# Two PSUM banks in turn for the last products of an expert slot, and a wait for the copy two slots behind

## The chip, the cores and the metric

The kernel runs on one core of a Trainium2 chip. Time is microseconds of one execution on the device. It is given as the median of three runs, and one further execution was profiled. TensorE is PE in the rows, VectorE DVE, ScalarE ACT, GpSimd POOL and SyncE SP.

## The reference, cut to what matters

Eight layers run over 4096 tokens of 128 numbers: a state-space layer, experts, landmark attention, the same experts again, causal attention, another set of experts, attention with a memory, and those experts again. The change touches the four expert layers. With 8 experts (the first two of them) each token takes two experts, with 4 experts (the last two) it takes one:

```python
g = jnp.einsum('bsh,ehi->ebsi', x, experts_w1)
u = jnp.einsum('bsh,ehi->ebsi', x, experts_w3)
hid = jax.nn.silu(g) * u                       # 512 numbers for a token and an expert
eo = jnp.einsum('ebsi,eih->ebsh', hid, experts_w2)
out = jnp.einsum('ebsh,bse->bsh', eo, tok_w)
```

## The kernel before

`expert_layer` computes only what the routing asks for. It sorts the tokens by expert into **slots** of 128 rows, each slot of one expert. An upper bound on their number is fixed: 71 slots in each of the first two expert layers, 35 in each of the last two, 212 in all. All numbers are fp32. Each engine has its own program and runs it in order. Semaphores tie them together. For slot n:

- POOL `gather(n)` (L575): an indirect DMA brings 128 token rows from DRAM into `xs`, six buffers deep. POOL issues the gather of slot n + 6 and then the scatter of slot n.
- PE `turn_rows(n)` (L725): one transpose of those rows into PSUM bank 4, issued two slots ahead. ACT `turned_rows` (L636) copies it to `xst`. ACT `up_weights(n)` (L649) copies the weights of the slot's expert, 128x1024, to `up_w`.
- PE `up(n)` (L733): the gate half into bank 0 or 1 and the other half into bank 2 or 3, four products of 128x128 each. The trace shows two matmul instructions for a product, so 16 for a slot.
- ACT `silu(n)` (L642) reads the first half, DVE `hidden(n)` (L856) multiplies it by the second into `hid`, two buffers deep.
- PE `rows(n)` (L741): the **last products**, 8 matmul instructions that add up in PSUM bank 5, columns 0 to 127. The semaphore `y_ready` tells of the last of them.
- DVE `rows(n)` (L862) copies bank 5 to one of four buffers `ys` and raises `y_copied`. Before it, DVE waits until the scatter of four slots back has landed (L861).
- POOL `scatter(n)` (L580) waits for `y_copied` and writes the rows to DRAM by an indirect DMA.

PE's order in its loop over n is: the waits for slot n's operands (`xst_ready`, `silu_ready` of slot n - 2, `up_copied`), the gate half, the other half, the transpose for slot n + 2, and the last products of slot n - 1. DVE's order is `hidden(n)`, then the copy of slot n - 1. ACT's order is `silu(n)`, the copy of the turned rows of slot n + 2, the weights of slot n + 2. When all slots are done, SP waits for the scatters, loads the results, and they are added to the tokens.

Banks 6 and 7 of the tensor `ps` hold the routing's numbers, which are all read before the first slot. In the slot loop they are unused.

Of the kernel before, what the change touches and what calls it, by code (L numbers as in the profile page):

```python
# [12 lines left out]
P = 128  # L13
# [417 lines left out]
def expert_layer(nc, g, name, experts, top, weights, gate_w, up_of, down, result=None):  # L431
# [8 lines left out]
    IB = 4  # L440
# [8 lines left out]
    XS, YS, WS = 6, 4, 3  # L449
    with ExitStack() as ctx:  # L450
# [16 lines left out]
        tiles, done, start = s.sb("tiles", [P, E]), s.sb("done", [P, E]), s.sb("start", [P, E])  # L467
# [14 lines left out]
        sg, hid = s.sb("sg", [P, 2, CHUNK]), s.sb("hid", [P, 2, CHUNK])  # L482
        up_w = s.sb("up_w", [P, WS, 2 * CHUNK])
        ys = s.sb("ys", [P, YS, P])
# [4 lines left out]
        ps = s.ps("ps", [P, 8, 512])  # L489
# [8 lines left out]
        S = {n: s.sem(n) for n in names}  # L498
# [19 lines left out]
        with nc.Block() as block:  # L518
# [151 lines left out]
            def _(pe):  # L670
# [39 lines left out]
                for k in range(K):  # L710
# [5 lines left out]
                    last = nc.tensor.matmul(ps_sums[:, k // NT, :], signs[:, k, :], coded[:, k, :], start=(k % NT == 0), stop=(k % NT == NT - 1))  # L716
# [10 lines left out]
                def expert_of(n):  # L727
                    return nc.values_load(table_e[0:1, n:n + 1], engines=(mybir.EngineType.PE,), min_val=0, max_val=E - 1,
                                          skip_runtime_bounds_check_because="table_e counts the experts that end before a slot and is cut at E - 1 by VectorE")
# [5 lines left out]

                def rows(n, e):
                    pe.wait_ge(S["hid_ready"], n + 1)
                    if n:
                        pe.wait_ge(S["y_copied"], n)
                    for j in range(IB):  # L740
                        last = nc.tensor.matmul(ps[:, 5, 0:P], hid[:, n % 2, j * P:j * P + P], down(e, j), start=(j == 0), stop=(j == IB - 1))  # L741
                    last.then_inc(S["y_ready"], 1)

                pe.wait_ge(S["table_ready"], 1)
# [2 lines left out]
                e, before = expert_of(0), None  # L747
                for n in range(SLOTS):
                    pe.wait_ge(S["xst_ready"], n + 1)
                    if n >= 2:  # L750
                        pe.wait_ge(S["silu_ready"], n - 1)
                    pe.wait_ge(S["up_copied"], n + 1)
                    up(n, 0, n % 2).then_inc(S["g_ready"], 1)
                    if n >= 2:
                        pe.wait_ge(S["hid_ready"], n - 1)
                    up(n, CHUNK, 2 + n % 2).then_inc(S["u_ready"], 1)
                    after = expert_of(n + 1) if n + 1 < SLOTS else None
                    if n + 2 < SLOTS:
                        turn_rows(n + 2)
                    if n:  # L760
                        rows(n - 1, before)
                    before, e = e, after
                rows(SLOTS - 1, before)

            @block.vector
            def _(dve):
# [3 lines left out]
                for c in range(NC_):  # L770
                    for t in range(c * CT, c * CT + CT):
                        last = nc.vector.tensor_scalar(xn[:, t, :], g.X[:, t, :], g.MV[:, t, 0:1], rstd[:, t:t + 1], ALU.subtract, ALU.mult)
# [35 lines left out]
                for r in range(top):  # L808
                    last = nc.vector.tensor_tensor(place[:, r], hot[:, r], rank[:].rearrange("p e t -> p t e"), ALU.mult)
# [48 lines left out]
                def rows(n):  # L858
                    dve.wait_ge(S["y_ready"], n + 1)
                    if n >= YS:  # L860
                        dve.wait_ge(y_stored[n % YS], n // YS * 16)  # L861
                    nc.vector.tensor_copy(ys[:, n % YS, :], ps[:, 5, 0:P]).then_inc(S["y_copied"], 1)  # L862

                hidden(0)
                for n in range(1, SLOTS):
                    hidden(n)
                    rows(n - 1)
                rows(SLOTS - 1)

                def fold(c):  # L870
# [1521 lines left out]
```

## Time and profile before

| | us |
|---|---|
| median of three runs | 2788.8 |
| lowest and highest | 2781.56, 2790.41 |
| the profiled execution, its own time | 2790.66 |
| span of that execution, first to last instruction | 2788.9 |
| PE busy (matmul), share of the span | 2227.6, 80% |
| DVE, ACT, POOL busy | 1813.1, 1398.5, 897.8 |
| mean granted clock of TensorE | 0.884 |

A busy time is the union of an engine's records. The four stretches in which the slot loops run are a quarter of the span; what the change does is read there. A duration of a matmul in the rows is from its start to its modelled end, and matmuls overlap: where they follow each other without a gap, one starts every 0.11 us or so, though each has 0.275 us in its record. So work on PE is better counted by starts than by busy time.

### The profile page before, as it was taken

To read this page: it belongs to the slowest core of one execution; us is meant where nothing else is said; L and a number is where in the kernel's file an instruction comes from. 1 tells how busy PE (TensorE), PEld (TensorE's weight loads), DVE (VectorE), ACT (ScalarE), POOL (GpSimd) and SP (SyncE) were. 2 spreads that over 40 slices of the span, in tenths; PEclk is the share of its full clock that TensorE was granted. 3 is DMA by queue.
4 is the path that set the end of the run, shared out by engine and by line. 5 is a ranking of instruction groups with operands and counts; after the bars stand their busy time and mean duration, and the time that the engine had idled before them with its cause. 6 is when DMAs were issued, how large, how long until landed. Compare 5 with 4: busy or idle time off the path is not lost. (4 is left out here: it accounts for less than half of the span.)

```text
span 2788.9 us, 78885 instructions
## 1 busy us (share of the span) xinstructions
PE 2227.6 (80%) x30447; PEld 1572.1 (56%) x30447; DVE 1813.1 (65%) x5841; ACT 1398.5 (50%) x3584; POOL 897.8 (32%) x904
## 2 busy tenths in 40 slices
PE   6499947699935888888888877948899888888686
PEld 3288835388812333333333335836777777777486
DVE  6633357633355776767867634359999999999622
ACT  5455543455521554454544445536556555555453
POOL 2156643166541101000000003534444444444254
PEclk7699979699965998988988887969999999999898
DMA  4111120111143211110110001121111111111112
GB/s 125 36 41 42 43 70 1 39 42 42 42 139 93 63 31 35 33 43 18 43 33 22 15 1 52 42 82 53 52 51 53 48 49 50 45 49 49 40 39 89
DMA packets 76684, 134.93 MB, mean 48 GB/s; under 512 B 17892, under 2 KB 32926, under 8 KB 73886
## 3 DMA queue, kind: packets, MB, share of 16 engines
q1 hardware_dynamic: 62742, 102.07, 11.6%
q0 software_dynamic: 13568, 27.81, 3.4%
q8 instruction: 250, 4.10, 0.6%
q14 instruction: 116, 0.95, 0.1%
q10 hardware_dynamic: 8, 0.00, 0.0%
HBM read 65.19 MB, written 32.79 MB: 35 GB/s over the span
## 5 line engine op out<-in xcount | busy, mean ns | idle before, releaser
L1499 ACT ACTIVATE ca_pt<-ca_ps 128x512 f32<-128x512 f32 (+3 forms) x768 | 341.9, 491 | 402.2 <-PE ca_ps L1601 198.8
L733 PE MATMUL ffn_ps<-ffn_xst,ffn_up_w 128*128 128x128 f32 x3392 | 420.6, 278 | 0.2 <-issue 0.2
L733 PEld LDWEIGHTS ffn_ps<-ffn_xst,ffn_up_w 128*128 128x128 f32 x3392 | 402.7, 195 | 1.2 <-issue 1.2
L856 DVE TENSOR_TENSOR ffn_hid<-ffn_sg,ffn_ps 128x512 f32<-128x512 f32 x212 | 145.8, 688 | 324.8 <-PE ffn_ps L733 234.3
L580 POOL DMA_INDIRECT ffn_y<-ffn_ys,ffn_result_at x212 | 208.8, 985 | 221.6 <-DVE ffn_ys L862 190.4
L1928 POOL TENSOR_TENSOR im_pt_e<-im_pt,im_own 128x512 f32<-128x512 f32 x128 | 162.6, 1271 | 361.9 <-DVE im_pt L2181 351.6
L575 POOL DMA_INDIRECT ffn_xs<-ffn_x,ffn_token_at x212 | 205.2, 968 | 229.7 <-DVE ffn_token_at L839 166.3
L1575 PE MATMUL ca_ps<-ca_stacks 72*128 72x512 bf16 (+3 forms) x768 | 233.3, 371 | 53.8 <-DVE ca_m_near L1721 28.2
L1597 PE MATMUL ca_ps<-ca_stacks 75*128 75x512 bf16 (+3 forms) x768 | 259.5, 361 | 16.8 <-ACT ca_pt L1499 11.2
L1720 DVE TENSOR_REDUCE ca_m_far<-ca_ps 128x1 f32<-128x128 f32 (+5 forms) x384 | 236.8, 617 | 49.7 <-PE ca_ps L1575 48.0
L1721 DVE CUSTOM_DVE_ANT_0 ca_spill<-ca_ps,ca_bias_q 128x256 f32<-128x256 f32 (+1 forms) x512 | 201.0, 397 | 32.5 <-PE ca_ps L1575 32.5
L1619 PE MATMUL ca_ps<-ca_pt,ca_vp 128*9 128x512 f32 (+3 forms) x1536 | 184.5, 555 | 41.6 <-ACT ca_ysb L1507 41.6
L642 ACT ACTIVATE ffn_sg<-ffn_ps 128x512 f32<-128x512 f32 x212 | 126.4, 596 | 139.4 <-PE ffn_ps L733 130.0
L1935 POOL TENSOR_TENSOR im_rope_qk<-im_t,im_mates 128x512 f32<-128x512 f32 x128 | 173.8, 1358 | 62.6 <-DMA im_mates<-im_t 61.7
L543 POOL MEMSET ffn_gate_wide<- 128x32 f32 x4 | 0.5, 125 | 593.4 <-POOLq L42 593.4
L741 PE MATMUL ffn_ps<-w_w,ffn_hid 128*128 x1136 | 156.3, 281 | 34.2 <-DVE ffn_ys L862 33.9
L1734 DVE TENSOR_TENSOR ca_ps<-ca_ps,ca_bias_kd 128x256 f32<-128x256 f32 (+1 forms) x288 | 109.9, 382 | 103.9 <-PE ca_ps L1597 100.0
L1575 PEld LDWEIGHTS ca_ps<-ca_stacks 72*128 72x128 bf16 x768 | 68.7, 104 | 191.1 <-DVE ca_m_near L1721 97.8
L862 DVE COPY ffn_ys<-ffn_ps 128x128 f32<-128x128 f32 x212 | 61.7, 291 | 161.0 <-remote 122.4
L741 PEld LDWEIGHTS ffn_ps<-w_w,ffn_hid 128*128 128x128 f32 x1136 | 137.8, 191 | 48.9 <-issue 48.9
L1961 ACT ACTIVATE im_ot<-im_ps 128x256 f32<-128x256 f32 x128 | 49.1, 383 | 228.8 <-PE im_ps L2024 228.8
L1597 PEld LDWEIGHTS ca_ps<-ca_stacks 75*128 75x128 bf16 x768 | 80.0, 104 | 145.9 <-ACT ca_pt L1499 72.0
(332 smaller groups left out, 4897.2 us busy)
## 6 DMA issues: line engine op xcount, KB each, us to landing
im_mates<-im_t SPq DMA_DIRECT2D x256, 128.0 KB
ca_stacks<-scratch_piece SPq DMA_DIRECT2D x96, 192.0 KB
ffn_got<-ffn_y SPq DMA_DIRECT2D x48, 256.0 KB, 5.4
ffn_x<-ffn_xn SPq DMA_DIRECT2D x32, 256.0 KB, 2.0
scratch_piece<-ca_piece SPq DMA_DIRECT2D x24, 256.0 KB, 2.9
w_w<-in_L_ffn_experts_w_dram SPq DMA_DIRECT2D x2, 2048.0 KB, 12.3
ffn_xs<-ffn_x,ffn_token_at POOLq DMA_INDIRECT x212
ffn_y<-ffn_ys,ffn_result_at POOLq DMA_INDIRECT x212
```

Source lines behind the costliest of these rows:

```text
L575: nc.gpsimd.indirect_dma_start(out=xs[:, n % XS, :], out_offset=None, in_=xn_rows[:, :], in_offset=bass.IndirectOffsetOnAxis(ap=token_at[: ...
L580: nc.gpsimd.indirect_dma_start(out=y_rows[:, :], out_offset=bass.IndirectOffsetOnAxis(ap=result_at[:, n:n + 1], axis=0), in_=ys[:, n % YS, ...
L733: last = nc.tensor.matmul(ps[:, bank, j * P:j * P + P], up_w[:, n % WS, first + j * P:first + j * P + P], xst[:, n % 2, :], start=True, st ...
L741: last = nc.tensor.matmul(ps[:, 5, 0:P], hid[:, n % 2, j * P:j * P + P], down(e, j), start=(j == 0), stop=(j == IB - 1))
L1499: nc.scalar.activation(pt[:, i % 8, lo - c0:hi - c0], ps[:, tile_bank(i), lo - c0:hi - c0], ACT.Exp, scale=SCALE).then_inc(p_ready, 1)
L1575: last = nc.tensor.matmul(slot_row(n)[:, c:e], stacks[0:KD, u % 3, 0, j, qt * P:qt * P + P], stacks[0:KD, u % 3, 1, j, c:e], start=True, s ...
L1597: last = nc.tensor.matmul(ps[:, tile_bank(i), lo - c0:hi - c0], stacks[:, u % 3, 1, j, kt * P:kt * P + P], stacks[:, u % 3, 0, j, lo:hi], ...
L1619: nc.tensor.matmul(ps[32 * j:32 * j + D + 1, 7, lo - c0:hi - c0], vp[:, b % 2, kt, gr * G4 + j, :], pt[:, i % 8, lo - c0:hi - c0], start=( ...
L1720: nc.vector.tensor_reduce(m_far[:, u % 2, t:t + 1], slot_row(n)[:, 0:lo], AX_X, ALU.max)
L1721: nc.vector.tensor_tensor_reduce(spill[:, n % 2, 0:hi - lo], slot_row(n)[:, lo:hi], bias_q[:, h, W2 - (hi - lo):W2], 1.0, NEG, ALU.add, AL ...
L1928: nc.gpsimd.tensor_tensor(pt_e[:, j % 2], pt[:].unsqueeze(2).to_broadcast(shape), own[:].unsqueeze(1).to_broadcast(shape), ALU.mult).then_ ...
L1935: nc.gpsimd.tensor_tensor(rope_qk[:, k % 2].rearrange("p a b -> p (a b)"), t1[:], mates[:, k % 2, :], ALU.subtract).then_inc(S["rope_ready ...
```

## The change

The last products of a slot go to bank 5 in even slots and to bank 6 in odd ones, VectorE's copy reads the same bank, and PE waits, ahead of the last products of slot n, for the copy of slot n - 2 instead of that of slot n - 1. Nothing else changes: no instruction is added or taken away except that slot 1 has no such wait.

```diff
                 def rows(n, e):
                     pe.wait_ge(S["hid_ready"], n + 1)
-                    if n:
-                        pe.wait_ge(S["y_copied"], n)
+                    if n >= 2:
+                        pe.wait_ge(S["y_copied"], n - 1)
                     for j in range(IB):
-                        last = nc.tensor.matmul(ps[:, 5, 0:P], hid[:, n % 2, j * P:j * P + P], down(e, j), start=(j == 0), stop=(j == IB - 1))
+                        last = nc.tensor.matmul(ps[:, 5 + n % 2, 0:P], hid[:, n % 2, j * P:j * P + P], down(e, j), start=(j == 0), stop=(j == IB - 1))
                     last.then_inc(S["y_ready"], 1)
...
-                    nc.vector.tensor_copy(ys[:, n % YS, :], ps[:, 5, 0:P]).then_inc(S["y_copied"], 1)
+                    nc.vector.tensor_copy(ys[:, n % YS, :], ps[:, 5 + n % 2, 0:P]).then_inc(S["y_copied"], 1)
```

## Rows read from the trace of the kernel before

**Rows 1.** Windows, the four slot loops: stretch, its length, busy (instructions), clock, DMA
```profile
core 0: us, PE busy (x) PEld busy (x) DVE busy (x) ACT busy (x) POOL busy (x), PEclk, DMA share, GB/s
136.00:361.20 225.20, 207.75 (x1773) 200.16 (x1773) 69.08 (x142) 128.69 (x211) 133.54 (x137) 0.99 0.14 41
547.20:774.00 226.80, 208.96 (x1774) 201.14 (x1773) 68.88 (x141) 128.89 (x211) 133.88 (x138) 0.99 0.15 41
1711.70:1822.50 110.80, 103.39 (x874) 99.95 (x873) 33.89 (x69) 63.15 (x103) 63.80 (x66) 0.98 0.14 40
2657.60:2768.70 111.10, 103.31 (x874) 99.63 (x873) 33.82 (x70) 63.14 (x103) 63.95 (x66) 0.98 0.14 40
```

**Rows 2.** Waits of the whole span: who waited for whom, total us, times, longest
```profile
POOL ffn_y L580 <- DVE ffn_ys L862: 190.4, 118, 3.9
...
DVE ffn_ys L862 <- remote: 122.4, 84, 2.2
...
PE ffn_ps L741 <- DVE ffn_ys L862: 48.5, 89, 0.9
```

**Rows 3.** Windows, two slots of the first loop and four at the end of the last
```profile
200.85:207.25 6.40, 5.84 (x50) 5.61 (x50) 1.96 (x4) 3.64 (x7) 3.91 (x4) 1.00 0.13 41
...
2754.80:2766.00 11.20, 11.19 (x100) 11.20 (x101) 3.92 (x8) 6.23 (x11) 4.82 (x5) 1.00 0.07 24
```

**Rows 4.** Timeline: start, length, engine, line, what, [idle before <- what ended it]
```profile
203.45 0.99 POOL L580 DMA_INDIRECT ffn_y<-ffn_ys,ffn_result_at  x1 [0.30 <-issue]
...
203.63 0.27 PE L725 MATMUL ffn_ps<-g_ident,ffn_xs 128*128 128x128 f32 x1
...
203.74 1.06 PE L741 MATMUL ffn_ps<-w_w,ffn_hid 128*128 x8
...
204.55 0.69 DVE L856 TENSOR_TENSOR ffn_hid<-ffn_sg,ffn_ps 128x512 f32<-128x512 f32 x1 [2.21 <-PE ffn_ps L733]
204.63 1.95 PE L733 MATMUL ffn_ps<-ffn_xst,ffn_up_w 128*128 128x128 f32 x16
204.74 0.97 POOL L575 DMA_INDIRECT ffn_xs<-ffn_x,ffn_token_at  x1 [0.30 <-issue]
205.21 0.28 ACT L636 ACTIVATE ffn_xst<-ffn_ps 128x128 f32<-128x128 f32 x1 [1.67 <-PE ffn_ps L725]
205.62 1.06 ACT L649 ACTIVATE ffn_up_w<-w_w 128x1024 f32 x1
...
206.42 0.27 PE L725 MATMUL ffn_ps<-g_ident,ffn_xs 128*128 128x128 f32 x1
206.72 0.29 DVE L862 COPY ffn_ys<-ffn_ps 128x128 f32<-128x128 f32 x1 [1.48 <-remote]
206.81 0.60 ACT L642 ACTIVATE ffn_sg<-ffn_ps 128x512 f32<-128x512 f32 x1
...
207.26 1.15 PE L741 MATMUL ffn_ps<-w_w,ffn_hid 128*128 x8 [0.56 <-DVE ffn_ys L862]
207.29 0.98 POOL L580 DMA_INDIRECT ffn_y<-ffn_ys,ffn_result_at  x1 [1.58 <-DVE ffn_ys L862]
...
207.44 0.69 DVE L856 TENSOR_TENSOR ffn_hid<-ffn_sg,ffn_ps 128x512 f32<-128x512 f32 x1 [0.43 <-ACT ffn_sg L642]
...
208.25 1.95 PE L733 MATMUL ffn_ps<-ffn_xst,ffn_up_w 128*128 128x128 f32 x16
208.45 0.29 DVE L862 COPY ffn_ys<-ffn_ps 128x128 f32<-128x128 f32 x1 [0.32 <-PE ffn_ps L741]
208.58 0.97 POOL L575 DMA_INDIRECT ffn_xs<-ffn_x,ffn_token_at  x1 [0.30 <-issue]
...
209.85 0.99 POOL L580 DMA_INDIRECT ffn_y<-ffn_ys,ffn_result_at  x1 [0.30 <-issue]
```

**Rows 5.** The chain that ended last, in order of time: start, length, what
```profile
2769.24 2.24 DMA ffn_y<-ffn_ys,ffn_result_at
```

## The prediction

> **What bounds the kernel now.** The page shows PE busy for four fifths of the span, so I looked for the stretches in which PE isn't full, and among them for those that the diff touches. Three views matter.
>
> The windows over the four slot loops [rows 1] show 225.2, 226.8, 110.8 and 111.1 us, together 673.9, with the TensorE clock granted at 0.98 to 1.00. PE is the busiest engine there: some 92% by its records, with POOL next at 59%. The clock isn't what holds PE back; something makes it stand still.
>
> The waits [rows 2] name it: PE's last products waited 89 times for VectorE's copy, 48.5 us in all. That is one wait in two of the 212 slots, leaving out the first and last few of each loop. It is the wait that the change loosens. The same view says that the copy itself was waited for by POOL's scatter (190.4 us) and that the copy waited 122.4 us for something called "remote", which can't be another core here.
>
> The windows of two slots and of four [rows 3] give the price. Fifty matmul instructions (two slots of 16 + 1 + 8) took 6.40 us in the steady state, 3.20 us a slot. At the end of the last loop, where no gathers are left and the wait doesn't occur, a hundred took 11.20 us, 2.80 us a slot, without a gap. That is PE's own pace: 0.112 us an instruction. So the idle 0.56 us in the timeline understates the wait; the restart's slower first instructions are a cost as well. A pair of slots loses 0.80 us.
>
> **Why the copy is late.** I name the slots by the last products: those at 203.74 in the timeline belong to slot n, those at 207.26 to slot n + 1 [rows 4]. Slot n's end at 204.80 (203.74 + 1.06) by their records. VectorE has been free since 205.24 (204.55 + 0.69), but its copy starts at 206.72. The "remote" is thus 1.9 us after the products' end by the records. The copy isn't alone. The transpose at 203.63 ended at 203.90 and ScalarE's copy of it starts at 205.21, 1.3 us late. The gate half of the products from 204.63 is over some 0.9 + 0.27 us later, at 205.8, and the silu on it starts at 206.81, 1.0 us late, just behind the copy. Everything that waits for PE is served late at this place, and at 206.7 it is served all at once. After that, slot n + 1's products end at 208.41 and its copy starts at 208.45 without delay.
>
> The POOL rows beside it [rows 4] run scatter (203.45), gather (204.74) without a pause, then stand idle for 1.58 us until 207.29. Then come scatter 207.29, gather 208.58, scatter 209.85 with 0.30 us between them. The late deliveries fall in the second half of four such issues in a row and end 1.0 us after the last of them (205.71 to 206.7). At the end of the last loop, with one issue a slot, there is none. I read this as: PE's signals are held back while POOL issues indirect DMAs densely, and let go when POOL pauses. The trace shows the coincidence, not the mechanism.
>
> This closes a circle of 6.40 us: four POOL issues of 0.98, 0.97, 0.98 and 0.97 us with 0.30 after each (5.1 us), plus 1.28 us of pause beyond the usual 0.30, which is the late signal, the copy (0.29) and its way to POOL (0.28). PE is tied into it by waiting for the same late copy.
>
> **The change, part by part.** Another bank for odd slots: the products and the copy keep their shapes, so 8 instructions of 0.112 us and 0.29 us stay; no instruction and no DMA is added. I put it at 0. Bounds: 0 below, since nothing gets shorter; above, 0.05 us a slot (10 us in all), as the spread of this copy's position against its releaser is not over that.
>
> The loosened wait: slot n + 1's products can start right behind the transpose of 206.42, at 206.53, if `hid` of slot n + 1 is there. It is, at 205.24. They then end at 207.42 instead of 208.25. That is 0.80 us earlier (0.73 of wait and about 0.1 of restart). What is late next? The up products behind them need the turned rows (ready 205.49) and weights (ready 205.62 + 1.06 = 206.68), both there 0.74 us ahead. One slot on, the last products of slot n + 2 would start at 209.32; their `hid` is made at 207.44 + 0.69 = 208.13, 1.19 us ahead, and the copy of slot n, for which they now wait, is done at 207.01. With the delays as they are, nothing takes the stall's place: 89 x 0.80 = 71 us. The loops' own sum agrees: 673.9 us less 212 x 2.80 = 593.6 is 80.3, and 71 of it leaves 2.3 us for the end of each of the four loops, where a silu (0.60), a product on VectorE (0.69) and the last products (1.06) follow each other uncovered. This is the upper bound of the gain.
>
> But the delays won't stay as they are. POOL needs 2.56 us a slot, PE 2.80. At full pace POOL would pause for 0.48 us in two slots beyond its 0.30s, not for 1.28. If the signals need POOL's pause to come through, it has to be taken at times. What changes is how often. Before, the pause came every two slots because slot n's late copy is what POOL itself waits for, and PE was held to that. With PE running on, its signals come 0.8 us earlier against POOL: in the second pair of rows the transpose would end at 209.5 instead of 210.3, ahead of the scatter of 209.85 that begins the dense part, and the last products of slot n + 2 at 210.5, before that scatter ends (210.84), instead of after it. So that copy can come early enough for POOL to go on without the pause. I take it that a pause of 1.28 us then comes every three or four slots instead of every two:
>
> - every two: (2 x 2.56 + 1.28) / 2 = 3.20 us, as now, gain 0;
> - every three: (3 x 2.56 + 1.28) / 3 = 2.99 us;
> - every four: (4 x 2.56 + 1.28) / 4 = 2.88 us;
> - none needed: PE's 2.80 us.
>
> 89 pairs are 178 slots. Three gives 178 x 0.21 = 37 us, four 178 x 0.32 = 57, none 71. I take the middle of three and four: **47 us less**. The work behind a loop (waiting for the scatters, loading results) starts that much earlier and keeps its length; no transfer of another layer overlaps the loops, so nothing collides with it. From the profiled execution's 2790.7 this gives 2743.7; the median of the runs is 1.9 us lower, so I forecast 2742 us.
>
> The Trainium skill has a rule that bears on the upper end: *Perfetto Trace Analysis*, Optimizing Tensor Performance, Matmuls, says that independent groups should rotate through PSUM banks so that the evacuation of one overlaps the next group's matmuls. By that rule the whole wait is hidden and the sum would be the 71 us; by the late signals in the rows it is 47.
>
> **Rivals.**
>
> *PE's pace reached in full* (57 to 75 us less, 2714 to 2732). For it: every margin above is positive with the delays of now. Against it: POOL gets denser.
>
> *A small gain* (9 to 37 us less): a pause in two slots remains in part of the loops and PE falls back into step.
>
> *POOL's circle stays at 6.40 us* (within 8 us, 2781 to 2797). If the copy that opens the pause stays as late as it is, POOL scatters two slots per 6.40 us, and PE, at most two slots ahead, ends up waiting for the copy of two slots back just as often. For it: the circle's four issues and its pause fill 6.40 us without needing PE's wait. Against it: the argument of the 210.5 above.
>
> *The copy waits for the scatter of four slots back*, the "remote" being a transfer. Then a second bank changes nothing. A scatter takes 2.24 us from issue to landing [rows 5], while four slots are 12.8 us, so this hardly can be; within 8 us.
>
> *Slower: denser POOL work delays the signals so far that ScalarE is late with the turned rows and weights.* The place is the start of the up products. The 1.3 us delay of the transpose's signal leaves 0.74 us. At 1.3 + 0.74 = 2.05 us of delay PE begins to lose, and from 2.85 us on it loses more than the 0.80 won. If a signal had to wait through one more scatter and gather (2.56 us), it would be 3.9 us late, PE would lose 1.8 us in two slots, 1.0 more than now: 89 us slower, 2878. With a delay just over the limit it is 10 to 30 us slower.
>
> *The clock.* It stands at 1.00 in both kinds of stretch [rows 3], with 0.56 us of idle time in two slots and with none. It would have to fall to its lower level, 1.2 GHz, for the change to lose by it; at half pace a slot of 2.80 us would take 5.6. PE becomes fuller, so I see no cause. The Trainium skill, *TensorE: Matmul & The Clock Gate*, A second HAM failure mode, tells of a kernel that cycled through PSUM banks and whose clock oscillated from small idle gaps between groups. By that rule the loops here would lose; the trace of before disagrees with it for gaps of 0.56 us.
>
> **How the numbers follow.** A measurement of this kernel tells a difference of about 0.3%, 8.4 us, from none. Chances: a pause every three or four slots 0.44, full pace 0.24, a small gain 0.08: faster 0.76. POOL's circle 0.13, the scatter 0.02: same 0.15. ScalarE late 0.08, clock 0.01: slower 0.09. The likeliest case alone runs from 2732 to 2752 (57 and 37 us less). The range reaches from the full pace, 2715 (71 us and the spread of the runs), to the edge of no change, 2781; what it leaves out is most of the same and slower cases, about 2 in 10.
>
> **What would show it.** The windows over the four loops should fall from 673.9 us to about 627 in sum, at an unchanged clock. PE's 89 waits of its last products for the copy should be all but gone; where they remain in number, POOL's circle is right. The copy's own wait (122.4 us) may remain, as late signals do; POOL's idle time before scatters should come in fewer and longer pieces than one in two slots. A new wait at the first up product for ScalarE would speak for the slower case. If POOL's busy share in the loops reaches 2.56 of 2.80 and its gaps are 0.30 us throughout, and signals are still not late, my reading of the delays is wrong.

## The result

| | median us | runs |
|---|---|---|
| before | 2785.1 | 20 |
| after | 2793.7 | 20 |

After stands to before as 1.0028, 95% interval 1.0015 to 1.0041: no gain, and a small loss of 0.15 to 0.4% that the interval tells from zero. I had forecast 2742 us, 47 us less than the 2788.8 us of the three runs that I had then.

The windows over the four slot loops of the kernel after, as in [rows 1]:

```profile
core 0: us, PE busy (x) PEld busy (x) DVE busy (x) ACT busy (x) POOL busy (x), PEclk, DMA share, GB/s
137.40:366.40 229.00, 212.67 (x1773) 207.36 (x1773) 66.45 (x141) 127.01 (x211) 133.21 (x137) 0.96 0.14 41
552.50:781.60 229.10, 212.44 (x1774) 207.63 (x1773) 66.50 (x142) 126.54 (x211) 133.59 (x138) 0.96 0.14 41
1726.80:1836.50 109.70, 103.19 (x874) 101.58 (x873) 32.72 (x69) 62.40 (x103) 63.55 (x66) 0.97 0.14 41
2659.20:2770.60 111.40, 104.14 (x874) 101.51 (x873) 32.51 (x69) 61.47 (x103) 63.55 (x66) 0.97 0.14 40
```

They sum to 679.2 us against 673.9, and the granted clock is lower in each: 0.96 and 0.97 against 0.98 and 0.99. POOL's busy time in them is the same.

The waits of the kernel after, beside [rows 2]:

```profile
POOL ffn_y L580 <- DVE ffn_ys L862: 192.5, 107, 3.8
...
DVE ffn_ys L862 <- remote: 73.1, 38, 2.7
...
ACT ffn_xst L636 <- remote: 56.9, 34, 2.4
...
DVE ffn_ys L862 <- PE ffn_ps L741: 53.2, 58, 3.0
...
PE ffn_ps L725 <- ACT ffn_xst L636: 36.9, 23, 2.4
```

The wait of the last products for the copy (48.5 us, 89 times) is gone from the list; the change did what it says. A wait of the transposes for ScalarE's copy stands in its place: fewer, 23, but 1.6 us each instead of 0.5. The copy still waits, 73.1 + 53.2 = 126.3 us; before it was 122.4 for "remote" and, in a row of that view not shown in [rows 2], 33.9 for L741. And POOL waits for the copy as long as before: 192.5 against 190.4 us.

The timeline of the kernel after shows how that comes about. Columns as in [rows 4]:

```profile
210.11 0.98 POOL L580 DMA_INDIRECT ffn_y<-ffn_ys,ffn_result_at  x1 [1.56 <-DVE ffn_ys L862]
...
216.45 0.98 POOL L580 DMA_INDIRECT ffn_y<-ffn_ys,ffn_result_at  x1 [1.52 <-DVE ffn_ys L862]
...
219.02 0.99 POOL L580 DMA_INDIRECT ffn_y<-ffn_ys,ffn_result_at  x1 [0.30 <-issue]
...
220.21 0.27 PE L725 MATMUL ffn_ps<-g_ident,ffn_xs 128*128 128x128 f32 x1
220.31 0.96 POOL L575 DMA_INDIRECT ffn_xs<-ffn_x,ffn_token_at  x1 [0.30 <-issue]
...
221.22 1.95 PE L733 MATMUL ffn_ps<-ffn_xst,ffn_up_w 128*128 128x128 f32 x16
221.58 0.99 POOL L580 DMA_INDIRECT ffn_y<-ffn_ys,ffn_result_at  x1 [0.30 <-issue]
222.24 0.60 ACT L642 ACTIVATE ffn_sg<-ffn_ps 128x512 f32<-128x512 f32 x1 [2.96 <-remote]
222.87 0.97 POOL L575 DMA_INDIRECT ffn_xs<-ffn_x,ffn_token_at  x1 [0.30 <-issue]
225.15 0.28 ACT L636 ACTIVATE ffn_xst<-ffn_ps 128x128 f32<-128x128 f32 x1 [2.31 <-remote]
225.17 0.69 DVE L856 TENSOR_TENSOR ffn_hid<-ffn_sg,ffn_ps 128x512 f32<-128x512 f32 x1 [5.58 <-remote]
225.57 0.36 PE L725 MATMUL ffn_ps<-g_ident,ffn_xs 128*128 128x128 f32 x1 [2.40 <-ACT ffn_xst L636]
225.78 0.28 DVE L862 COPY ffn_ys<-ffn_ps 128x128 f32<-128x128 f32 x1
226.00 2.07 PE L741 MATMUL ffn_ps<-w_w,ffn_hid 128*128 x8
226.34 0.99 POOL L580 DMA_INDIRECT ffn_y<-ffn_ys,ffn_result_at  x1 [2.50 <-DVE ffn_ys L862]
```

The transpose at 220.21 is over at 220.48; ScalarE reads it at 225.15, 4.7 us later, where before the longest such delay in the rows was 1.9. The delay sits at the end of six POOL issues with 0.30 us between them (216.45 to 222.87) instead of four. After four such issues POOL paused 1.56 and 1.52 us (the rows of 210.11 and 216.45), as before; after six it pauses 2.50. These 2.50 us are the late signal (1.33, from 223.84, the end of the last issue, to 225.17), VectorE's product, which was held up too and now stands ahead of the copy (0.61), and the copy and its way (0.56).

From 210.11 to 226.34 five scatters begin: 16.23 us, 3.25 us a slot, as before (3.20). POOL got its issues out in a longer run and then paid with a longer pause.

That holds for the loops as a whole. Leaving out their first 6 and last 22 us, the kernel before has 82 runs of four issues with a pause of 1.56 us behind them on average, and 3 runs of two. The kernel after has 54 runs of four with 1.60 us, 18 of six with 2.47, and 2 of two. A run of six comes to (6 x 1.28 + 2.47 - 0.30) / 3 = 3.28 us a slot, a run of four to 3.21. PE's idle time in the loops stays as well: 46.5 us against 48.1, now in 32 pieces instead of 88 (those over 0.25 us).

Two windows of the kernel after show what a pause of that length does to the clock, beside [rows 3]:

```profile
219.00:225.50 6.50, 4.17 (x38) 3.97 (x36) 0.62 (x2) 1.16 (x3) 3.91 (x4) 1.00 0.17 50
225.70:229.10 3.40, 3.33 (x15) 3.11 (x15) 1.34 (x4) 2.52 (x4) 2.15 (x3) 0.50 0.08 24
```

Behind this standstill of PE the clock is granted at 0.50, its lower level, 1.2 GHz, and 15 instructions start in 3.4 us where 30 would. From the mean clocks, an estimate: the loops spent 2 x (0.04 x 458.1 + 0.03 x 221.1) = 50 us at that level after, and 2 x (0.01 x 452.0 + 0.02 x 221.9) = 18 us before. The difference of 32 us costs up to half of itself, 16 us.

The granted clock in the two traces agrees: inside the loops after there are ten falls of 3.41 us each, 34 us, and inside those before none. Each of the ten begins behind a standstill of 1.36 to 2.40 us. Four other standstills of 1.9 to 2.4 us have no fall behind them, so length alone doesn't decide. By this estimate the loosened wait won up to 11 us in the loops, and the clock took them and 5 more.

### The profile page after: what moved, and what is told of

Read it like the earlier page. It is cut to its first block and busy times, and to the rows that moved or that the text cites. A ratio compares the mean times of both kernels' runs of the same rounds, so it can differ in the third digit from the quotient of the medians.

```text
span 2791.3 us, 78881 instructions
## 1 busy us (share of the span) xinstructions
PE 2234.9 (80%) x30447; PEld 1584.0 (57%) x30447; DVE 1801.4 (65%) x5841; ACT 1392.8 (50%) x3584; POOL 898.6 (32%) x904
## 2 busy tenths in 40 slices
DMA packets 76684, 134.93 MB, mean 48 GB/s; under 512 B 17892, under 2 KB 32926, under 8 KB 73886
## 5 line engine op out<-in xcount | busy, mean ns | idle before, releaser
L733 PE MATMUL ffn_ps<-ffn_xst,ffn_up_w 128*128 128x128 f32 x3392 | 433.7, 282 | 4.9 <-issue 4.3
L733 PEld LDWEIGHTS ffn_ps<-ffn_xst,ffn_up_w 128*128 128x128 f32 x3392 | 414.3, 199 | 6.9 <-issue 6.9
L580 POOL DMA_INDIRECT ffn_y<-ffn_ys,ffn_result_at x212 | 208.9, 985 | 227.1 <-DVE ffn_ys L862 192.5
L1721 DVE CUSTOM_DVE_ANT_0 ca_spill<-ca_ps,ca_bias_q 128x256 f32<-128x256 f32 (+1 forms) x512 | 200.8, 397 | 33.9 <-PE ca_ps L1575 33.9
L741 PE MATMUL ffn_ps<-w_w,ffn_hid 128*128 x1136 | 157.4, 283 | 2.9 <-DVE ffn_hid L856 0.5
L649 ACT ACTIVATE ffn_up_w<-w_w 128x1024 f32 x142 | 150.0, 1058 | 15.9 <-DVE ffn_table_e L828 3.6
L1975 ACT ACTIVATE im_pe_<-im_s,im_nm 128x32 f32<-128x32 f32 x512 | 157.0, 316 | 1.7 <-DVE im_nm L2190 1.7
```

The source lines that it names most:

```text
L580: nc.gpsimd.indirect_dma_start(out=y_rows[:, :], out_offset=bass.IndirectOffsetOnAxis(ap=result_at[:, n:n + 1], axis=0), in_=ys[:, n % YS, ...
L733: last = nc.tensor.matmul(ps[:, bank, j * P:j * P + P], up_w[:, n % WS, first + j * P:first + j * P + P], xst[:, n % 2, :], start=True, st ...
L741: last = nc.tensor.matmul(ps[:, 5 + n % 2, 0:P], hid[:, n % 2, j * P:j * P + P], down(e, j), start=(j == 0), stop=(j == IB - 1))
L1721: nc.vector.tensor_tensor_reduce(spill[:, n % 2, 0:hi - lo], slot_row(n)[:, lo:hi], bias_q[:, h, W2 - (hi - lo):W2], 1.0, NEG, ALU.add, AL ...
```

## The experiments

The chips turned out to differ, so each group of runs is told with the time of the kernel before on its own chip. Ratios are to that kernel.

### First chip: take an issue off POOL, or loosen one more wait. Before: 2713.5 us (27 runs)

In the no-scatter kernels POOL's scatters are made by SyncE, in slot order:

```diff
@@ POOL
                     gather(n + XS)
-                    scatter(n)
@@ SyncE, after the stores of xn
+                for n in range(SLOTS):
+                    sp.wait_ge(S["y_copied"], n + 1)
+                    sp.dma_start(y_rows[n * P:n * P + P, :], ys[:, n % YS, :]).then_inc(y_stored[n % YS], 16)
```

> The kernel before, with the scatters taken off POOL: SyncE writes each slot's rows to DRAM by a plain DMA of the same size, in slot order, so the results land at other places than the reference's. POOL issues only the gathers. Theory A (PE's signals are held back while POOL issues gathers and scatters densely): no late signals, PE's 89 waits of the last products for the copy vanish, a slot takes 2.80 us, the four loops 673.9 us fall to about 603, the kernel is 70 us faster. Rival B (the copy is late for a reason of its own: PE, bank 5, or VectorE): the pairs of slots stay at 6.40 us and the time within 8 us.

Measured: 2709.4 us, ratio 1.000 (0.998 to 1.002).

> The changed kernel with the same edit (scatters by SyncE as plain DMAs in slot order, results at other places). Theory A: the same 2.80 us a slot and 70 us less than the kernel before, equal to the run above within 5 us: with the delays gone the wait is hidden by one bank already and the change is worth nothing. Rival C (the change itself costs, through bank 6 or the order): slower than the run above by 10 us or more.

Measured: 2720.5 us, 1.0023 (1.0003 to 1.0043). The up products of the four loops run over 591.7 us in sum here and over 592.0 in the run above, so the 0.2% isn't in the part that the change touches.

```diff
@@ POOL
-                for n in range(XS):
-                    gather(n)
...
-                    if n + XS < SLOTS:
-                        gather(n + XS)
                     scatter(n)
@@ SyncE
+                    if n >= XS:
+                        sp.wait_ge(S["x_turned"], n - XS + 1)
+                    sp.dma_start(xs[:, n % XS, :], xn_rows[n % NT * P:n % NT * P + P, :]).then_inc(xs_loaded[n % XS], 16)
```

> The changed kernel with the gathers taken off POOL: SyncE loads rows of the normalized tokens by plain DMAs in token order, so wrong tokens are computed on. POOL issues only the scatters. Theory A, any dense POOL issues do it: one issue of 1.28 us in 2.80 is sparse, no late signals, 70 us less than before. Rival D (the scatters alone are the cause, gathers are innocent): the signals stay late beside each scatter and the loops stay over 640 us.

Measured: 2708.5 us, 0.998 (0.995 to 1.000).

```diff
-                    if n:
-                        pe.wait_ge(S["xst_ready"], n)
-                    nc.tensor.transpose(ps[:, 4, 0:P], xs[:, n % XS, :], g.ident[:]).then_inc(S["x_turned"], 1)
+                    if n >= 2:
+                        pe.wait_ge(S["xst_ready"], n - 1)
+                    nc.tensor.transpose(ps[:, 4 + n % 2 * 3, 0:P], xs[:, n % XS, :], g.ident[:]).then_inc(S["x_turned"], 1)
```

> The changed kernel, with the transposes in banks 4 and 7 in turn and PE waiting, ahead of a transpose, for ScalarE's copy two slots behind. In the changed kernel PE's idle time stands before the transposes (36.9 us in 23 waits for that copy). Theory A (POOL needs its pauses, PE is held to POOL's circle through one wait or another): the waits move on again, to the up products or the last products, and the time stays within 10 us of the changed kernel. Rival E (the wait for the turned rows simply took the other's place): PE runs at its pace, the loops fall from 679 us to about 620, and the kernel is 50 to 70 us faster.

Measured: 2714.6 us, 1.001 (0.9995 to 1.003).

All four land between 2708 and 2721 us, near the 2713 of the kernel before. None of the expectations was met as put, for the ground was another: this chip runs the kernel before 72 us faster than the chip of the result. Nothing could be told about the causes here, except that 72 us is what I had put down for the waits (71).

### Second chip: both kernels again, traced. Before: 2715.4 us (17 runs)

> The kernel before, unchanged, for its trace beside its time on this chip. The chip of the four runs so far ran it in 2713 us, 72 us less than the 2785 us of the comparison of the two kernels, which is just what the held-back signals cost there by my sum (71 us). Theory F (the held-back signals belong to some chips and not to others): where the time is near 2713 us the four loops sum to about 592 us, 2.80 us a slot, without waits of the last products; where it is near 2785 us, 674 us in pairs of 6.40. Rival G (the chips differ elsewhere, in clock or memory): loops near 674 us in either case.

Measured: 2713.6 us. The windows over its loops:

```profile
136.20:336.00 199.80, 199.22 (x1769) 199.04 (x1770) 69.26 (x141) 135.64 (x211) 132.92 (x137) 0.99 0.16 47
523.50:724.00 200.50, 199.92 (x1768) 199.74 (x1768) 69.09 (x141) 135.96 (x211) 133.16 (x138) 0.99 0.17 46
1668.00:1768.50 100.50, 99.92 (x874) 99.52 (x873) 34.00 (x69) 66.33 (x103) 64.00 (x66) 0.98 0.15 45
2590.40:2690.00 99.60, 99.02 (x871) 98.76 (x871) 34.00 (x69) 66.32 (x103) 63.41 (x66) 0.98 0.15 45
```

600.4 us against 673.9, PE busy for all but 2 us. These windows end 2.1 us, in all, ahead of the last products; from the first up product to the end of the last products the four loops take 602.5 us here and took 673.7. Its timeline:

```profile
203.06 1.06 PE L741 MATMUL ffn_ps<-w_w,ffn_hid 128*128 x8
...
204.16 0.29 DVE L862 COPY ffn_ys<-ffn_ps 128x128 f32<-128x128 f32 x1 [0.26 <-PE ffn_ps L741]
204.73 0.98 POOL L580 DMA_INDIRECT ffn_y<-ffn_ys,ffn_result_at  x1 [0.53 <-DVE ffn_ys L862]
```

The products end at 204.12 and the copy starts 0.04 us later. The traces record when a semaphore is updated, so this can be counted. PE updates four semaphores in a slot (`x_turned`, `g_ready`, `u_ready`, `y_ready`), 848 times in the four loops, and here all 848 updates lie within 0.1 us of the end of their instruction. In the trace of the kernel before that the prediction was made from, only 292 do, and `y_ready` for the products that end at 204.80 [rows 4] is updated at 206.70, just ahead of the copy at 206.72. The same program, instruction for instruction, has no held-back signal here. Theory F holds as far as this goes: they came on one chip and not on another. Whether it is the chip, or something of the machine at that time, isn't shown.

> The changed kernel, unchanged. Theory F: on a chip without held-back signals the wait for the copy is hidden by one bank already, so before and after are the same within 0.3%, with loops of 592 us in both. On a chip with them: again 0.1 to 0.4% slower, loops near 679 us.

Measured: 2717.6 us, ratio 1.0008 (0.9987 to 1.0028): the same, as expected.

> The kernel before with the scatters made by SyncE as plain DMAs in slot order (results at other places). Theory A (dense POOL issues hold PE's signals back): on a chip that shows held-back signals this falls to loops of 592 us, 70 us or more below the kernel before; on a chip without them it says nothing, as the run of this kernel so far (2709 against 2713 us). Rival B: on a chip that shows them, the loops stay near 674 us.

> The changed kernel with the transposes in two banks as well, PE waiting for ScalarE's copy two slots behind. On a chip with held-back signals: theory A says POOL's circle keeps the loops at 660 to 680 us; rival E says they fall to about 620 us. On a chip without them 592 us, as before.

Measured: 2711.5 us, and 2730.9 us in one run each; the second's loops are as fast as the others' (591.4 us by the same count), so its 15 us lie outside them. No news.

### Third chip: a late copy by a fixed amount. Before: 2710.8 us (4 runs), no held-back signals

```diff
                 def rows(n):
+                    if n % 2 and n < SLOTS - 2:
+                        for k in range(3):
+                            t = (n // 2 % 2 * 3 + k) * 4
+                            nc.vector.tensor_copy(got[:, 0, t:t + 4, :], ps[:, 7, :].rearrange("p (t d) -> p t d", d=P))
                     dve.wait_ge(S["y_ready"], n + 1)
```

> The kernel before, with VectorE copying bank 7 three times into unused space ahead of the copy of every odd slot, some 1.9 us, so that this copy is late by about as much as the held-back signals made it, and by a fixed amount. On a chip without held-back signals, theory A (my sum of one late copy in two slots is right for a delay that stays as it is): PE waits for the copy in every pair and a pair takes 6.2 to 6.4 us instead of 5.58, the four loops 650 to 675 us instead of 592, the kernel 60 to 80 us slower than before. Rival H (such a late copy is hidden by other slack): under 20 us slower.

Measured: 2751.7 us (2 runs), ratio 1.015 (1.012 to 1.018): 41 us slower. From its timeline:

```profile
199.95 1.06 PE L741 MATMUL ffn_ps<-w_w,ffn_hid 128*128 x8
...
202.50 0.28 DVE L866 COPY ffn_ys<-ffn_ps 128x128 f32<-128x128 f32 x1
...
203.03 1.15 PE L741 MATMUL ffn_ps<-w_w,ffn_hid 128*128 x8
203.06 0.99 POOL L580 DMA_INDIRECT ffn_y<-ffn_ys,ffn_result_at  x1 [1.14 <-DVE ffn_ys L866]
...
204.35 0.97 POOL L575 DMA_INDIRECT ffn_xs<-ffn_x,ffn_token_at  x1 [0.30 <-issue]
...
205.63 0.99 POOL L580 DMA_INDIRECT ffn_y<-ffn_ys,ffn_result_at  x1 [0.31 <-issue]
...
206.92 0.96 POOL L575 DMA_INDIRECT ffn_xs<-ffn_x,ffn_token_at  x1 [0.30 <-issue]
207.90 0.60 ACT L642 ACTIVATE ffn_sg<-ffn_ps 128x512 f32<-128x512 f32 x1 [0.30 <-PE ffn_ps L733]
```

The copy is late by 1.5 us (202.50 against 201.01), not 1.9, since the three extra copies begin before the products end. The pair takes 203.03 to 209.00, 5.97 us. That is 0.39 us over PE's 5.58, and the 100 pairs with such a copy give 39 us. The size was below my expectation because the delay was; the mechanism is as put. The rows show one thing more. POOL has four issues with 0.30 us between them here, as densely as in [rows 4], and ScalarE's silu at 207.90 comes on time. So dense issues alone don't hold signals back on every chip. The numbers of the traces agree: all 848 updates of PE are prompt here too.

> The changed kernel with the same late copies. Theory A: the second bank hides a fixed delay of 1.9 us: loops within 8 us of 592, the time of the kernel before, so some 70 us under the run above. Rival I (the loosened wait only hands the loss to the next wait, whatever the cause of the delay): it is as slow as the run above within 15 us.

Measured: 2696.2 us (3 runs), ratio 0.997 (0.992 to 1.003); its loops take 599.8 us by the windows, the run above 641.1. A fixed delay is hidden in full by the second bank. Rival I falls.

> Once more the kernel before with SyncE's plain DMAs in place of the scatters (results at other places), in case this chip shows held-back signals. If it does (kernel before near 2785 us): theory A says 2713 us here, rival B 2785. If it doesn't: 2713 us for both, which tells nothing.

> Once more the changed kernel with the transposes in two banks as well. On a chip with held-back signals: theory A 2780 to 2795 us, rival E 2720 to 2740. On one without: 2713 us, no news.

Measured: 2711.4 and 2721.4 us in one run each, no news on this chip.

### Fourth chip: a late copy that hangs on POOL's issues. Before: 2786.5 us (3 runs), with held-back signals

```diff
                 def rows(n):
+                    if n % 2 == 0 and n + XS < SLOTS:
+                        dve.wait_ge(xs_loaded[(n + XS) % XS], ((n + XS) // XS + 1) * 16)
                     dve.wait_ge(S["y_ready"], n + 1)
```

> Once more the kernel before with SyncE's plain DMAs in place of the scatters (results at other places), for the case that this chip shows held-back signals (kernel before near 2785 us). Then theory A says 2713 us, rival B 2785. Otherwise 2713 us for both, no news.

Measured, in one run: 2714.4 us, against 2786.5 (2778.1 to 2789.3): 72 us less. The windows over its loops:

```profile
137.80:338.50 200.70, 199.52 (x1770) 199.08 (x1771) 69.17 (x141) 135.34 (x211) 62.69 (x67) 0.99 0.17 46
525.60:727.50 201.90, 200.43 (x1770) 199.73 (x1770) 69.01 (x141) 135.45 (x211) 63.65 (x68) 0.99 0.18 46
1665.60:1766.70 101.10, 100.07 (x874) 99.70 (x873) 33.82 (x69) 66.25 (x103) 29.58 (x32) 0.98 0.17 45
2591.80:2693.00 101.20, 99.85 (x873) 99.17 (x873) 33.81 (x69) 66.26 (x103) 29.64 (x32) 0.98 0.17 44
```

With the scatters off POOL the loops run close to PE's pace (606.6 us from the first up product to the last products, against 602.5 on the second chip) on the chip that holds signals back, with one bank and the old wait. The DMA queues move as many bytes, 134.93 MB; what is gone is POOL's second indirect DMA in a slot. Rival B falls: the late copy came from POOL's issues, not from PE, the bank or VectorE.

The same trace also tells the density of the issues from the mix of two kinds, for no scatter is left on POOL. At the start of each loop POOL issues its gathers without a pause, nine in a row in the first loop (132.40 to 142.56), and there the signals are late:

```profile
141.24 1.95 PE L735 MATMUL ffn_ps<-ffn_xst,ffn_up_w 128*128 128x128 f32 x16
...
142.56 0.94 POOL L578 DMA_INDIRECT ffn_xs<-ffn_x,ffn_token_at  x1 [0.30 <-issue]
143.03 0.27 PE L727 MATMUL ffn_ps<-g_ident,ffn_xs 128*128 128x128 f32 x1
...
145.00 0.60 ACT L644 ACTIVATE ffn_sg<-ffn_ps 128x512 f32<-128x512 f32 x1 [2.11 <-remote]
...
145.50 0.27 ACT L638 ACTIVATE ffn_xst<-ffn_ps 128x128 f32<-128x128 f32 x1
```

The gate half from 141.24 is over near 142.4 and its silu starts at 145.00, 1.5 us after the last of the nine issues ends. Of PE's 848 updates 808 are prompt, and the 40 others all lie in the first 12 us of a loop. Afterwards, with one gather in 2.79 us, none is late. So gathers alone hold the signals back on this chip where they are dense, and don't where they are sparse: theory A is shown for gathers. Dense scatters alone weren't run on such a chip.

> The kernel before, with VectorE's copy of every even slot n waiting also for the landing of the gather of slot n + 6, the last one that POOL issues before it needs that copy. That builds, on a chip without held-back signals, a delay that follows POOL's issues as those signals did: POOL's circle is scatter, gather, scatter (3 x 1.28 us), a gather and its landing (2.6 us from its issue on this chip), the copy and its way (0.6 us): some 7.0 us for two slots, loops of 720 to 740 us in place of 592, the kernel 130 to 150 us slower than before.

Measured: 2850.8 us (2 runs), ratio 1.024 (1.014 to 1.033); loops 741.7 us.

> The changed kernel with the same wait. Theory J (what my prediction missed: a late copy that hangs on POOL's own issues closes a circle without PE, and a second bank can't shorten it): the same time as the run above within 8 us, with PE's idle time before other instructions. Rival K (the second bank hides this delay as it hid the fixed one): 40 us or more faster than the run above.

Measured: 2846.5 us (2 runs), ratio 1.022 (1.017 to 1.028); loops 730.8 us. The two differ by 4 us in the time and 11 us in the loops. Theory J holds, rival K falls. The expectations were made for a chip without held-back signals, whose kernel before takes 2713 us; against that it is 138 us slower, within the 130 to 150. On this chip PE's signals are held back beside it (of `y_ready`'s 212 updates 120 and 117 are prompt), but a pair of slots takes 7.0 to 7.2 us in both, the sum of the built-in circle, so the late signals set nothing. The built-in delay hasn't been run on a chip without them. The traces also show why the second bank doesn't help. The copy of a pair starts 2.6 us after the issue of the gather it waits for in both kernels (205.25 after 202.63, 207.02 after 204.43). Against its own products it is 2.6 us late with one bank and 4.8 with two: they end earlier, and the copy doesn't move. Where PE stands, from the waits of the kernel before and of the changed one with this circle, the row in which its last products wait:

```profile
PE ffn_ps L741 <- DVE ffn_ys L864: 113.9, 95, 2.5
```

and with two banks:

```profile
PE ffn_ps L741 <- DVE ffn_hid L856: 105.6, 84, 2.4
```

With one bank PE waits for the copy; with two it waits, at the same instruction, about as long, for `hid`, which VectorE makes only after the copy that it is held at. The wait changed its name and kept its length.

### Fifth chip: what of POOL's issues does it. Before: 2713.4 us (15 runs), no held-back signals

The pairs kernel issues two gathers, then two scatters:

```diff
-                for n in range(SLOTS):
-                    if n + XS < SLOTS:
-                        gather(n + XS)
-                    scatter(n)
+                for n in range(0, SLOTS, 2):
+                    for k in (n, n + 1):
+                        if k + XS < SLOTS:
+                            gather(k + XS)
+                    for k in (n, n + 1):
+                        if k < SLOTS:
+                            scatter(k)
```

> The changed kernel with the transposes in two banks as well. On a chip with held-back signals (kernel before near 2785 us): theory A (POOL needs its pauses and PE is held to its circle through one wait or another) 2770 to 2800 us, the waits before the transposes gone and others in their place; rival E (the wait for the turned rows simply took the other's place) 2720 to 2745 us. On one without: 2713 us.

> The changed kernel with SyncE's plain DMAs in token order in place of the gathers (wrong tokens are computed on); POOL issues the scatters alone, one in a slot. On a chip with held-back signals: if density does it, none are late and it takes 2710 us, as with the gathers alone; if the scatters themselves do it, over 2750 us.

> The kernel before, with POOL issuing two gathers and then two scatters in place of one and one in turn; as many issues in the same time. On a chip with held-back signals: if density does it, 2775 to 2800 us, with the pause still once in four issues; if the change from one kind to the other does it, half as many delays and 2730 to 2755 us. On one without: 2713 us within 8.

Measured: 2712.4 us, 1.000 (0.998 to 1.002); 2707.6 us; 2718.2 us, 1.002 (1.000 to 1.004). The chip didn't hold signals back, so these runs leave their three questions open; the trace with the scatters off POOL above answers one of them in part.

## Why the prediction was wrong, point by point

**PE's pace and the price of the wait: right.** 2.80 us a slot and 71 us for the waits. On the first of the chips without late signals the kernel before takes 72 us less, and on the second its loops take 602.5 us against 673.7.

**Signals held back while POOL issues indirect DMAs densely: right, for chips that do it.** It was read off a coincidence; the no-scatter kernel on such a chip shows it, late while gathers come densely and prompt while they don't. I hadn't thought of the chip as a condition.

**The loosened wait hides a delay that stays as it is: right.** b_late and a_late show it: 41 us lost with one bank, nothing with two. The rival that the copy waits for an older scatter falls by the traces too: where signals aren't held back, the copy starts 0.04 us after the products, and where they are, it starts 0.02 us after the late update of `y_ready` (206.72 and 206.70).

**"I take it that a pause of 1.28 us then comes every three or four slots instead of every two": the step that failed.** I let the pause keep its size and stretched what lies between. In the kernel after, a run of four issues is still followed by a pause of some 1.5 us (1.2 to 1.3 beyond the usual 0.30), and a run of six by 2.5. The longer runs did come, 18 times, with 2.2 us of pause beyond the usual 0.30 in place of my 1.28: 3.28 us a slot where my sum had 2.99. POOL's average stays at 3.2 us a slot. My argument for it was that slot n + 2's products would end at 210.5 (209.32 and 1.06 give 210.4), before the scatter that ends at 210.84, and that the signal would then get through. The trace after has such a case and says otherwise: the transpose of 220.21 ended ahead of the scatter of 221.58 and was seen at 225.15. What bounds the loop is a circle of POOL's issues, the held-back signal, VectorE's copy and POOL again. PE's wait was tied to it, not a part of it. This was my third rival, "POOL's circle stays at 6.40 us", to which I gave 0.13; its own sentence ("the circle's four issues and its pause fill 6.40 us without needing PE's wait") was the right reading. It was wrong on where PE would stand: not at the last products, for the copy of two slots back, but ahead of the transposes. So my sign for this rival, that the 89 waits remain in number, would have misled: they are gone, and the circle stayed. The circle runs on the fourth chip show that such a circle is not shortened by a second bank.

**"The 1.3 us delay of the transpose's signal leaves 0.74 us": right for the delays shown, and overtaken.** The margin was 2.05 us of delay in all; the delays grew to 4.7 us, and PE stood before the transposes, one instruction earlier than I had looked. That is the growth of delays of my rival of the late ScalarE (3.9 us, chance 0.08). It came 23 times and not at each of 89 pairs, so it cost nothing like the 89 us that I had put on it.

**The clock: the rival that I gave 0.01.** I asked whether many small gaps would slow it, and they don't. The change gathered them into fewer, longer ones, 2.40 us in the row shown, and behind ten of those over 1.3 us the clock is at 0.50. By my estimate it cost up to 16 us and turned a small gain in the loops into a small loss; no run took the clock by itself. The Trainium skill, *TensorE: Matmul & The Clock Gate*, A second HAM failure mode, puts the cost of idling between groups in such falls; by that rule the loops would lose, and the trace after agrees (0.96 and 0.97), though the cycling through banks isn't the cause: a_late cycles through the same two banks at 0.98 and 0.99, without PE's standstills.

The range ended at the edge of no change, 2781, and left "same" and "slower", 24 in 100 by my own chances, outside. The result lies there.

**Open.** Why PE's signals are held back on some chips and not on others, whether that stays with a chip, and by what path POOL's indirect DMAs reach them. Whether dense scatters alone do what dense gathers alone do. Whether one more loosened wait (the transposes in two banks) would help on such a chip. No version that computes the reference was found that beats the kernel before; taking the scatters off POOL is worth 72 us on a chip with held-back signals, but as run it leaves the rows in slot order, and bringing them back costs gathers that weren't tried.

## What to carry to other kernels

Before loosening a wait, follow the late thing back to its source and ask whether the source depends on the waiting engine at all. If the delay comes round through another engine's own queue (here POOL to signal to copy to POOL), more buffers for the waiting engine only move its idle time and gather it into longer pieces, which may cost clock besides. Where many consumers of one engine start late at the same moment, look at what else runs then, and run the kernel on another chip before building on it.

## What the runs showed of the hardware

- In the comparison of the two kernels (2785 us) and on the fourth chip (2786 us; it may be the same one) PE's signals reach VectorE and ScalarE late, up to 4.7 us in the rows shown, while POOL issues indirect DMAs with 0.30 us between them, gathers alone included. On the four other chips (2711 to 2715 us) the traces show them within 0.1 us, in b_late at the same density. The difference for this kernel is 72 us, 2.6%.
- On a chip that does it, the delays end about 1 us after the last of POOL's issues (205.71 to 206.7 before, 223.84 to 225.1 after), and with one gather in 2.8 us there are none (e_b_noscatter).
- The label "remote" stood for such a signal on a one-core program: an update at a time at which the profile knows of no instruction that ends.
- Ten standstills of PE of 1.36 to 2.40 us were each followed by 3.41 us at half the clock, four others of 1.9 to 2.4 us weren't; nor were gaps of 0.56 us, one in 6.4 us.
